# Output projection of a cross-attention and state-space block: the projection runs three groups ahead instead of five, the normalised tile has two buffers, and each group is normalised ahead of the copies of the group before it

## The reference, cut to what matters

```python
x = _layernorm(builder_state, g1, beta1)                 # [4096, 512]
base_n = _layernorm(base_state, g1, beta1)               # [3202, 512]
x = residual + _mha(x, base_n, W_qkv, b_qkv, W_o, b_o)   # ends with out @ W_o.T + b_o
residual = x
xn = _layernorm(x, g2, beta2)
U = (xn @ W_in.T + b_in) @ Bmat                          # [4096, 64]
# scan over the 4096 tokens: s = silu(s @ A.T) + u_t
ssm_out = states @ Cmat
x = residual + ssm_out
mod = program_probs.mean(axis=1) @ W_prog.T + b_prog
return x + mod[:, None, :]
```

## Time and profile before

| | |
|---|---|
| median of 3 runs | 2342.01 us (2337.03 to 2344.16) |
| the profiled execution | 2339.71 us |
| its span, from first to last instruction | 2337.9 us |
| granted TensorE clock, mean | 0.985 |
| PE busy over the span | 2267.2 us (97%) |
| DVE, ACT, POOL busy | 1727.7, 1117.8, 1584.2 us |

### The profile page before, as it was taken

The page is one execution under the profiler, slowest core; times in us unless marked ns, Lnnn a source line. Parts: engine busy times, 40 slices in busy tenths (PEclk is TensorE's granted clock), DMA queues, the critical chain, the costliest instruction groups (busy, mean ns, idle before and its releaser), DMA issues.

```text
span 2337.9 us, 35932 instructions
## 1 busy us (share of the span) xinstructions
PE 2267.2 (97%) x14134; PEld 1311.6 (56%) x14134; DVE 1727.7 (74%) x2167; ACT 1117.8 (48%) x1422; POOL 1584.2 (68%) x1039
## 2 busy tenths in 40 slices
PE   8999989999999999999999999999999999998977
PEld 8998854455555545555555555555555555445754
DVE  5865546788888877878888888887888888746835
ACT  3654423544544444545544544544544454451454
POOL 1200026888888888888888888888888888886301
PEclk9999999999999999999999999999999999999978
DMA  6650225676767777767767777767767777787613
GB/s 242 217 180 10 82 72 118 150 159 156 157 154 155 173 168 173 169 153 162 159 153 178 176 172 163 160 159 157 159 152 156 158 155 159 180 183 196 211 63 144
DMA packets 158678, 365.01 MB, mean 156 GB/s; under 512 B 22511, under 2 KB 62063, under 8 KB 157870
## 3 DMA queue, kind: packets, MB, share of 16 engines
q0 software_dynamic: 59904, 218.13, 45.7%
q1 hardware_dynamic: 98606, 144.58, 19.1%
HBM read 95.41 MB, written 49.02 MB: 62 GB/s over the span
## 4 chain that ended last, share of the span: by engine, by line
PE 90%; DMA 3%; DVE 3%; issue 1%; ACT 1%; POOL 1%; SPq 0%; DVEq 0%; ACTq 0%; POOLq 0%
PE ps L1309 31%; PE ps L1182 11%; PE ps L1284 8%; PE ps L1286 8%; PE ps L1288 8%; PE ps L1146 4%; PE ps L1276 4%; PE ps L1164 3%; PE ps L1154 3%; PE ps L1373 3%; DMA acca<-pt 3%; PE ps L1127 1%; PE ps L1319 1%; DVE mx_part L921 1%; PE ps L1430 1%
## 5 line engine op out<-in xcount | busy, mean ns | idle before, releaser
L716 ACT ACTIVATE pt<-ps 128x1024 f32<-128x1024 f32 x800 | 779.3, 1021 | 910.2 <-PE ps L1288 887.3
L921 DVE TENSOR_REDUCE mx_part<-ps 128x2 f32<-128x1024 f32 x768 | 938.2, 1222 | 350.2 <-PE ps L1182 350.2
L534 POOL TENSOR_TENSOR accp<-accp,pt 128x1024 f32<-128x1024 f32 x416 | 1037.6, 2494 | 233.0 <-ACT pt L716 230.6
L1309 PE MATMUL ps<-pt,v 128*64 128x512 f32 x3328 | 807.0, 606 | 0.0
L994 DVE TENSOR_TENSOR ps<-ps,shb 128x1024 f32<-128x1024 f32 x403 | 493.2, 1224 | 50.8 <-PE ps L1288 50.8
L1309 PEld LDWEIGHTS ps<-pt,v 128*64 128x64 f32 x3328 | 202.1, 136 | 345.0 <-issue 335.1
L1182 PE MATMUL ps<-kk,qh 64*128 64x512 f32 x1536 | 349.2, 451 | 10.0 <-DVE mx_part L921 10.0
L1182 PEld LDWEIGHTS ps<-kk,qh 64*128 64x128 f32 x1536 | 143.3, 183 | 367.8 <-DVE mx_part L921 266.1
L1284 PE MATMUL ps<-qh,kk 64*128 64x512 f32 x1664 | 327.8, 390 | 4.4 <-ACT pt L716 4.4
L1286 PE MATMUL ps<-qh,kk 64*128 64x512 f32 x1664 | 328.2, 390 | 0.0
L1288 PE MATMUL ps<-ql,kk 64*128 64x512 f32 x1664 | 327.7, 389 | 0.0
(11 more groups left out here) (154 smaller groups left out, 1922.3 us busy)
## 6 DMA issues: line engine op xcount, KB each, us to landing
acca<-pt POOLq DMA_DIRECT2D x224, 512.0 KB, 4.9
accb<-pt POOLq DMA_DIRECT2D x160, 512.0 KB, 4.7
q_scratch<-kk SPq DMA_DIRECT2D x32, 512.0 KB, 4.4
acca<-accp POOLq DMA_DIRECT2D x32, 512.0 KB, 4.6
o_scratch<-ost SPq DMA_DIRECT2D x32, 512.0 KB, 3.0
og<-o_scratch SPq DMA_DIRECT2D x32, 512.0 KB, 5.7
shb<-m_scratch SPq DMA_DIRECT2D x31, 512.0 KB, 4.1
xs<-x SPq DMA_DIRECT2D x16, 512.0 KB, 6.4
```

Source lines behind the costliest of these rows:

```text
L534: nc.gpsimd.tensor_tensor(acc[:, :], acc[:, :], pt[n % PT_SLOTS][:, :], ALU.add).then_inc(added_p, 1)
L716: nc.scalar.activation(pt[n % PT_SLOTS][:, :], src, ACT.Exp, scale=SCALE).then_inc(exped, 1)
L921: nc.vector.tensor_reduce(mx_part[:, m % QT, :, m // QT], src, AX_X, ALU.max).then_inc(max_taken, 1)
L1309: ins = mm(ps[HD * h:HD * (h + 1), 6, :], v[:, t, f:f + HD], pt[n % PT_SLOTS][:, h * QB:(h + 1) * QB], start=(t == 0), stop=(t == NT - 1))
```

## The change

It alters the order of the same work, and the buffers between its steps:

- PE projects three groups before the loop and three ahead in it (`OG_SLOTS` in place of `AHEAD`), so that the loop projects up to d = 12.
- `xn` gets two buffers; `work` moves by 1024 elements to make room. ACT does `norm2(0)` before its loop and `norm2(d + 1)` as the first step of turn d, ahead of `take_u` and `take_n2(d)`; `norm2` waits for the turn of two groups before, in place of one.
- `LN_SLOTS` is 4 in place of 6.
- DVE takes the groups in plain order: `add_x(0)`, `norm2_scale(0)`, `add_x(1)`, and so on (one function `project`).
- The steps of the last attention unit move by up to two turns of their loops: `fold_den` from d = 8 to 6, the inversion from 7 to 5, `spread_rden` from 11 to 9, `scale_o` from 11 to 10, `high_o` from 5 to 6, `low_o` from 13 to 12. On PE the two small matmul groups of the mean move from d = 6 and 8 to 8 and 10, where they again follow the projections of groups 11 and 13.

```diff
-AHEAD = 5
-LN_SLOTS = 6
+LN_SLOTS = 4
...
-        xn = at("xn", [P, GT, H], 36368)
-        work = at("work", [P, 1024], 37392)
+        xn = at("xn", [P, 2, GT, H], 36368)
+        work = at("work", [P, 1024], 38416)
...
-                if d == 8:
+                if d == 6:
                     fold_den(UNITS - 1)
...
-                if d == 11:
+                if d == 9:
                     spread_rden(UNITS - 1)
...
-                if d == 11:
+                if d == 10:
                     scale_o(UNITS - 1)
-                if d == 13:
+                if d == 12:
                     low_o(UNITS - 1)
...
             def norm2(d):
                 act.wait_ge(ln2_ready, d + 1)
-                wait(act, n2_turned, 2 * d)
+                wait(act, n2_turned, 2 * (d - 1))
                 for t in range(GT):
-                    ins = nc.scalar.activation(xn[:, t], x1(d)[:, t], ACT.Identity,
+                    ins = nc.scalar.activation(xn[:, d % 2, t], x1(d)[:, t], ACT.Identity,
...
+            norm2(0)
             for d in range(X_G):
-                norm2(d)
+                if d + 1 < X_G:
+                    norm2(d + 1)
                 if d > 0 and d % 2 == 0:
                     take_u(d // 2 - 1)
                 take_n2(d)
                 if d == 0:
                     take_den(UNITS - 1)
-                if d == 5:
+                if d == 6:
                     high_o(UNITS - 1)
...
-            add_x(0)
             for d in range(X_G):
-                if d == 0:
-                    add_x(1)
-                if d > 1:
-                    add_x(d)
-                norm2_scale(d)
-                if d == 7:
+                project(d)
+                if d == 5:
                     invert(UNITS - 1)
...
-            for d in range(AHEAD):
+            for d in range(OG_SLOTS):
                 project(d, 0)
                 project(d, 1)
             for d in range(X_G):
-                if d + AHEAD < X_G:
-                    project(d + AHEAD, 0)
+                if d + OG_SLOTS < X_G:
+                    project(d + OG_SLOTS, 0)
                 if d > 0 and d % 2 == 0:
                     finish(d // 2 - 1)
-                if d + AHEAD < X_G:
-                    project(d + AHEAD, 1)
+                if d + OG_SLOTS < X_G:
+                    project(d + OG_SLOTS, 1)
                 turn2(d)
                 if d == 0:
                     spread_sum(UNITS - 1)
-                if d == 6:
+                if d == 8:
                     pe.wait_ge(cb_summed, 1)
...
-                if d == 8:
+                if d == 10:
                     pe.wait_ge(mean_ready, 1)
```

More of the change, by code:

```diff
@@ L228, in build @@
         yb = small[:, 24:26]
-        nmr = at("nmr", [P, LN_SLOTS, GT], RR + 11792)
+        nmr = at("nmr", [P, LN_SLOTS, GT], RR + 11784)
         cu = [small[0:SD, 30:31], small[SD:2 * SD, 30:31]]
@@ L272, in build @@
         bound = work[0:SD, 768:768 + NCH]
-        excess = xn[0:SD, 0, 0:NCH]
+        excess = xn[0:SD, 0, 0, 0:NCH]
         u_tokens = u_low.rearrange("p (k c) -> p c k", c=NCH)
@@ L1030, in _, with project @@
                         nc.vector.tensor_tensor(bo[:, :], ps[:, 4, :], bo[:, :], ALU.add).then_inc(bo_ready, 1)
-            def add_x(d):
+            def project(d):
                 dve.wait_ge(xb_ready, d + 1)
@@ L1038, in add_x @@
                         .then_inc(x1_ready, 1)
-            def norm2_scale(d):
                 dve.wait_ge(x1_ready, GT * (d + 1))
@@ L1382, in turn2 @@
                         ins = nc.tensor.transpose(ps[:, 4 + c // 2, (c % 2) * GW + t * P:(c % 2) * GW + (t + 1) * P],
-                                                  xn[:, t, c * P:(c + 1) * P], ident[:, :])
+                                                  xn[:, d % 2, t, c * P:(c + 1) * P], ident[:, :])
                     if c % 2:
```

## The result

The changed kernel takes 2325.11 us (median of 4 runs, 2322.50 to 2325.37), the kernel before 2342.91 (4 runs, 2337.03 to 2344.16): a ratio of 0.9926, 95% interval 0.9908 to 0.9945. That is 17.8 us faster; 18.4 were forecast, and 2323 us.

What follows compares the result with a forecast made beforehand. PE was taken as the bound mid-stage, waits on DVE at the start and an ACT-PE chain at the end. Gains of 4.3 + 3.1 + 11.0 = 18.4 us gave 2323 us, range 2314 to 2332 (8 in 10).

Steps and rivals of the forecast that it cites:

- The end: ACT-PE chain closing the projection stage: 34.2 us becomes 3.7 ahead of the last projection's end plus 19.5 behind, 11.0 gained.
- The start: PE's early waits for DVE: loss of 6.8 us in place of 11.1, so 4.3 us gained.
- each POOL addition holds up one tiny instruction: First scale and shift on DVE, beside POOL: held-up instructions make it 9 us in place of 4, ending at 2135.4.
- The clock's term: After PE's first long wait the granted clock falls, and the slower matmuls cost 1.6 us more.
- The middle: Waits near the mean and group 12: 1.5 us in place of 4.6, so 3.1 gained, somewhere between 0 and 4.6.
- one POOL hit: Steady groups on DVE: at most one POOL addition seems to hit, costing 1.1 us; DVE's work then takes 6.5 us.
- PE waits for DVE in steady groups: Sign in the new trace that would show the forecast wrong; about 1.5 us of loss a group would make the kernel slower.
- a matter of bunched transfers: Last denominator's round trip holds SP 4.9 us, so bias additions hit group 11's scale and shift; `spread_rden` at d = 9 shifts this.
- The middle hitch stays: Rival: DVE's extras still meet POOL's additions and the start gains nothing; only the end's 11 us remain, 2331 us, chance 0.17.
- DVE as the bound: Rival: three POOL hits a group give DVE 8.8 us against PE's 7.4; 20 us slower, 2362 us, chance 0.03.
- An end that isn't shortened: Rival: something unseen bounds ACT's chain, so only order changes; within 7 us of before, 2337 to 2345 us, chance 0.05.
- The clean start: Rival: DVE isn't held, PE's wait at the start goes and the clock stays up; 2317 down to 2313 us, chance 0.15.

Runs made afterwards that it cites:

- the second profile: The unaltered changed kernel measured and profiled once more, on the same chip as three other runs; 2323.43 us, ratio 0.9926 to the kernel before, stage 142.6 us.
- e_stats_behind: Changed kernel with DVE's scale and shift one group behind, the next group's bank emptied first, `cb_sum`, mean and scaled-output wait one turn earlier; 2316.60 us, ratio 0.9906.
- the lead alone: Kernel before with PE projecting three groups ahead and its two mean steps moved along, all else old; 2344.16 us, ratio 1.0017.
- the Silu last: Changed kernel with the scan's starting Silu and its table load moved on ACT from turn 12 to behind the last copies; 2324.35 us, ratio 0.9935.

## Why the prediction was right

*The end.* Forecast 19.5 us behind the last projection, measured 19.4; 11.0 us gained, as forecast, with ACT's steps in the order that was worked out. On this chain both finishes (3.46 and 3.68 us) and the last turn (1.94) did run at the lower clock. The runs bear out the parts: 22.6 us with one buffer, where 22.5 was expected, and 27.4 with the buffer and the old lead, where about 29 was.

*The start.* The step that reads rows 4 to 6 as "each POOL addition holds up one tiny instruction" held to 0.2 us, and 4.79 us of wait stand against 5.2. The clock's term was undersized: 48 matmuls took 13.92 us, 2.85 more than the 11.07 of the full clock, not 1.6; in the second profile it was 13.18, or 2.1 more. Loss 7.6 in place of 6.8, gain 3.5 in place of 4.3. With the additions two columns wide, all but 0.36 us of the wait and all of the clock loss are gone, so POOL's additions are shown to be the cause.

*The middle.* The term that was mis-sized. I put 1.5 us of waits there, and 3.3 came (0.58 + 0.47 + 0.58 + 1.30 + 0.41). The clause "one POOL hit" for a steady group was wrong in groups 4, 5, 7, 9 and 13: `xb` lands while DVE's tiny instructions still run, and both additions hit. Behind groups 5, 7 and 9 PE's next projection then starts late. DVE and POOL in the changed kernel, ahead of PE's wait at 2173.71:

```profile
2170.44 1.22 DVE L860 SCALAR_TENSOR_TENSOR ya<-small,ya 128x2 f32<-128x2 f32 x1
2171.69 1.20 DVE L862 SCALAR_TENSOR_TENSOR nmr<-small,ya 128x2 f32<-128x2 f32 x1
```

```profile
2170.36 2.52 POOL L578 TENSOR_TENSOR xb<-xb,bo 128x512 f32<-128x512 f32 x2 [5.98 <-DMA xb<-x]
```

The run with narrow additions has none of these waits but the 0.41. Against 4.6 us of before, or 5.0 with the 0.41 that I hadn't listed, the idle column gives a gain of 1.7. It leaves out a part of each wait behind a turn: a projection usually starts 0.79 us after the turn before it, here 2173.71 - 2172.09 = 1.62 us after it, with only 0.58 in the column. Counted from the start of the first turn to the end of the last projection, the middle takes 2246.24 - 2164.16 = 82.1 us before and 2245.52 - 2149.72 = 95.8 after, with two projections, two turns and a finish more in it, 11.1 + 3.7 us of work. So the middle gained 1.1 us and not 3.1.

*The sum.* 3.5 + 1.1 + 11.0 = 15.6, which is what the stage shows; the second profile of the change has 17.8, and the medians give 17.8 and, in the second measurement, 17.2. The forecast of 18.4 is above all of these, and that the medians come within 0.6 us of it, where the first profile's parts miss by 2.8, is partly luck. Two of the prediction's own signs of being wrong did appear: PE waits for DVE in steady groups, and the last projection ends at 2245.5 where 2242 was written. Both stand for the same shortfall of about 3 us ahead of the end. It was covered by the range, and the end, the largest term, was right by its mechanism.

*What the text had wrong without paying for it.* The moves of the last unit's steps stand in it as a matter of bunched transfers, worth some 3 us near group 12. The runs show another and larger purpose: turn d of ACT's loop now meets an earlier group, and `high_o` left in turn 5 stops ACT for 16.5 us. The old places cost 7.2 us; 4.4 of them go when `high_o` alone is moved later, and only the remaining 2.8 (5.0 against the second profile of the change) can be the bunching. Even of that a part seems to have another cause. In the kernel before, a third tiny instruction of group 11 is held up, right behind the two that the bias additions hold, and what holds it is POOL's `low_o` (L574):

```profile
2218.88 1.26 POOL L574 TENSOR_TENSOR ost<-oraw,ost 128x512 fp32r<-128x512 f32 x1
2218.97 1.19 DVE L861 SCALAR_TENSOR_TENSOR nmr<-small,ya 128x2 f32<-128x2 f32 x1
```

That is 1.0 of the 1.84 us that PE waits for `x1` of group 12. With the old places and `high_o` late the same three are held, and PE waits 1.83 us. In the changed kernel `low_o` starts at 2211.61, beside `cb_sum`, and no tiny instruction is held by it. No run moves `low_o` alone.

Of `high_o` I wrote that it might wait 3 us where the change puts it; it waits for nothing, as the row shows, which starts as the copies before it end. The margin is small: POOL's `scale_o` ended at 2198.31, 0.3 us before.

```profile
2197.51 1.09 ACT L764 ACTIVATE nt<-ps 128x512 f32<-128x512 f32 x2 [0.99 <-PE ps L1376]
2198.63 0.63 ACT L730 ACTIVATE ost<-oraw 128x512 fp32r<-128x512 f32 x1
```

*The rivals.* The middle hitch stays: its wait of 1.84 us is gone, and the start did gain, though the middle gained only 1.1. DVE as the bound: in the new middle PE waits about half a microsecond for DVE three times, far from the 1.5 us a group that would have made it slower. An end that isn't shortened: it went from 34.0 to 19.4. The clean start didn't come by the change; it is what `e_stats_behind` buys by order alone.

Left open: why these additions begin 3.6 to 3.7 us behind the `x1` of such a group, where in the steady groups of the kernel before most began 3.8 to 4.4 us behind it; a few tenths decide between one hit and two. It wasn't tried.

## What to carry to other kernels

When the lead of one engine's loop over another's is changed, every step placed by a loop index moves against the data it waits for. List them, and for each ask which group its producer stands behind; here one such line was worth more than the change of the lead. A bank that the matmul engine waits for is better emptied before a long chain of tiny instructions than after it, as the run with scale and shift one group behind shows. And the length of such a chain depends on the neighbour engine: here a 0.17 us instruction took as long as the addition beside it.

## What the runs showed of the hardware

A DVE instruction of 128x2 with one SBUF input took 2.29 us where it met a POOL addition of 128x1024. Beside additions of 128x512 such instructions took 1.2 us, with one SBUF input (L853 at 2133.50 in the kernel before) as with two; undisturbed they take 0.16 or 0.17. `cb_sum`, a reduction that began in the changed kernel just as POOL's 1.29 us of `low_o` did, took 3.06 us, where it took 3.08 in the kernel before, begun while POOL stood still; it was not held up. POOL's 128x512 bias additions cost the stage 12.2 us in all (10.0 against the second profile), though POOL itself waits 66.3 of its 144.9 us for transfers. The attention ahead of the stage, the same program in all kernels, put the first projection anywhere from 2116.8 us (the lead alone) to 2125.0 us (the Silu last) after the start of the span, so that a difference of a few microseconds between two spans says nothing of the stage, which has to be read by itself.
